# Elementwise steps of a four-layer network moved from VectorE and ScalarE to GpSimd, with the hand-written instruction order rewritten

## What is computed

```python
# layers 0 and 1: causal attention, a sign-weight linear, then a mixture of 16 experts (top 2) and a shared one
x = x + L2_xattn(ctx, layernorm(x), mask)    # query, key and value are each layer-normed after their projection:
    query = layernorm(q @ Wq + bq) * qn_scale + qn_bias     # key and value alike
x = x + L2_ffn(layernorm(x))                 # _bitlinear: rows scaled to 127 / max|row|, rounded, clipped
    xq = clip(round(x * scale), -128, 127) / scale
    hidden = silu(bitlinear(x, w_gate)) * bitlinear(x, w_up);  out = bitlinear(hidden, w_down)
x = x + L3_xattn(layernorm(x), ctx, ctx)     # keys and values are ctx itself, no projection
for blk in range(3):                         # L3_ffn, on h = layernorm(x)
    w = (q / 7.5 - 1.0) * scale              # 4-bit weights, a scale for each 16 of them, plus a low-rank term
    h = linear(gelu(layernorm(linear(h)) * gamma + beta)) + h
```

## Time and profile before

| | |
|---|---|
| median of three runs | 1198.68 us (1193.59 to 1200.58) |
| the profiled execution | 1198.55 us |
| its span, first to last instruction | 1196.6 us |
| busy: TensorE, VectorE, ScalarE, GpSimd | 1067.9, 945.9, 826.6, 488.3 us |
| as shares of the span | 89%, 79%, 69%, 41% |
| mean granted clock of TensorE | 0.972 of full speed |

### The profile page before, as it was taken

The page is one execution under the profiler, slowest core; times in us unless marked ns, Lnnn a source line. Parts: engine busy times, 40 slices in busy tenths (PEclk is TensorE's granted clock), DMA queues, the critical chain, the costliest instruction groups (busy, mean ns, idle before and its releaser), DMA issues.

```text
span 1196.6 us, 26279 instructions
## 1 busy us (share of the span) xinstructions
PE 1067.9 (89%) x8350; PEld 796.2 (67%) x8406; DVE 945.9 (79%) x3207; ACT 826.6 (69%) x1560; POOL 488.3 (41%) x1027
## 2 busy tenths in 40 slices
PE   6998999999999988899999988798899999988876
PEld 4676777777887765666677765366576766656654
DVE  3898888878555788877967798999999989898732
ACT  5777666657665666365667667457889798979953
POOL 6233356653122457657601144233334433423334
PEclk9999999999999999888999998999999999999988
DMA  7885332226777245303587752222203212121000
GB/s 221 260 275 180 87 101 71 85 76 189 218 211 213 89 121 140 85 14 116 150 259 229 233 167 80 56 69 82 82 19 87 72 54 81 53 63 54 10 10 18
DMA packets 102326, 140.03 MB, mean 117 GB/s; under 512 B 12336, under 2 KB 79792, under 8 KB 102192
## 3 DMA queue, kind: packets, MB, share of 16 engines
q1 hardware_dynamic: 99120, 129.97, 37.3%
q0 software_dynamic: 3072, 8.39, 2.2%
HBM read 65.43 MB, written 22.54 MB: 74 GB/s over the span
## 4 chain that ended last, share of the span: by engine, by line
PE 48%; DVE 20%; ACT 11%; DMA 7%; issue 6%; POOL 4%; SPq 3%; another core or an unknown queue 0%; DVEq 0%; ACTq 0%; POOLq 0%
PE ps L1516 10%; PE ps L1637 5%; PE ps L1536 4%; PE ps L1554 4%; PE ps L1729 4%; PE ps L1509 3%; DVE neg_max L2200 3%; PE ps L1523 3%; DVE ps L2196 3%; ACT probs L1945 3%; PE ps L1696 2%; DMA w<-in_expert 2%; ACT q_st L1960 2%; PE ps L1736 2%; DVE bn L2077 2%
## 5 line engine op out<-in xcount | busy, mean ns | idle before, releaser
L1945 ACT ACTIVATE probs<-ps 128x384 f32<-128x384 f32 (+1 forms) x512 | 263.5, 543 | 68.0 <-PE ps L1557 32.3
L1536 PE MATMUL ps<-k_st,q_st 96*128 96x256 bf16 (+1 forms) x1024 | 178.8, 265 | 19.4 <-DVE neg_max L2196 9.7
L1554 PE MATMUL ps<-q_st,k_st 104*128 104x256 bf16 (+1 forms) x1024 | 179.2, 263 | 14.8 <-ACT q_st L1960 6.7
L2200 DVE TENSOR_REDUCE neg_max<-ps 128x2 f32<-128x512 f32 x256 | 168.0, 679 | 11.7 <-PE ps L1536 4.9
L1960 ACT ACTIVATE q_st<-ps 8x1024 bf16<-8x1024 f32 x128 | 130.1, 1016 | 42.3 <-PE ps L1619 39.4
L2517 POOL TENSOR_SCALAR var_eps<-mv 128x2 f32<-128x2 f32 (+1 forms) x115 | 29.0, 252 | 298.0 <-DVE mv L2080 286.9
L2196 DVE CUSTOM_DVE_ANT_0 ps<-ps,diag_s 128x128 f32<-128x128 f32 (+1 forms) x384 | 123.3, 357 | 24.1 <-PE ps L1536 23.4
L1536 PEld LDWEIGHTS ps<-k_st,q_st 96*128 96x128 bf16 x1024 | 88.4, 100 | 70.3 <-DVE neg_max L2196 17.5
L1554 PEld LDWEIGHTS ps<-q_st,k_st 104*128 104x128 bf16 x1024 | 90.9, 99 | 60.3 <-issue 16.3
L1637 PE MATMUL ps<-probs,v 128*32 128x256 f32 (+1 forms) x2048 | 123.0, 359 | 4.7 <-ACT probs L1945 2.8
L2542 POOL CAST parts<-qf 128x512 bf16<-128x512 f32 x64 | 39.1, 612 | 205.2 <-DVE qf L2094 101.9
(11 more groups left out here) (270 smaller groups left out, 2545.8 us busy)
## 6 DMA issues: line engine op xcount, KB each, us to landing
k_st<-parts SPq DMA_DIRECT2D x192, 128.0 KB
q_st<-parts SPq DMA_DIRECT2D x192, 128.0 KB
w<-in_expert SPq DMA_DIRECT2D x62, 384.0 KB, 3.9
x_rows<-wo SPq DMA_DIRECT2D x10, 768.0 KB, 7.1
ctx_t<-in_ctx_t SPq DMA_DIRECT2D x16, 256.0 KB, 3.0
ring<-x_rows SPq DMA_DIRECT2D x31, 128.0 KB, 3.9
y_rows<-ring SPq DMA_DIRECT2D x31, 128.0 KB, 3.8
xn_t<-x_rows SPq DMA_DIRECT2D x31, 128.0 KB, 3.4
```

The source lines that it names most:

```text
L1536: last = mm(t[:, c0:c0 + n], head(q_st, r, h, KROWS, j * P, P), head(k_st, r, h, KROWS, 0, n), start=j == 0 or L != 2, stop=L != 2, skip_g ...
L1554: last = mm(t[:, j * S:j * S + n], head(k_st, r, h, KALL, j * P, P), head(q_st, r, h, KALL, skip, n), start=j == 0 or L == 3, stop=L == 3, ...
L1945: nc.scalar.activation(probs[:, (hg % 2) * HPG + h4, 0:width], tile_of(key)[:, 0:width], ACT.Exp, scale=SCALE).then_inc(*tile_drained(key))
L2200: V.tensor_reduce(neg_max[:, hg, h4, :], tile_of(key).rearrange("p (j t) -> p j t", j=SJ), AX.X, ALU.max, negate=True).then_inc(*tile_drai ...
```

## The change

Six things are moved to GpSimd, each with the same arithmetic: the norms of L2's queries, keys and values and of the blocks of the last feed-forward part (from ScalarE), and from VectorE the two rounding instructions of `quantise` and of `hidden_quant`, the two multiplications of `lora_add`, `value_scale`, and the values of layer 3. The moved steps get lanes' steps of their own (`quantise_round`, `hidden_round`, `lora_scale`, `v_copy`) and semaphores of their own (`ln_made`, `xq_round`, `hid_round`, `lora_made`). `low_load` waits for the last four expert tiles in place of the last one, and the first block that reads the 4-bit weights, whichever batch it belongs to, waits for them. The whole table `AT` is written anew, from the first microseconds on; it now ends at 1128.9 us.

```diff
 AT = (
...
 def low_rank(part):
...
         part.lora(n)
         yield
+        part.lora_scale(n)
+        yield
         part.lora_add(n)
...
     part.quantise(b)
     yield
+    part.quantise_round(b)
+    yield
     part.quantised(b)
...
     part.hidden_quant(T)
     yield
+    part.hidden_round(T)
+    yield
     part.down_turn(T)
...
     part.ctx_load(b)
     yield
-    part.v_take(3, b)
+    part.v_copy(3, b)
...
                 def block_in(n, b):
                     t = claim(pe, ("y", n, b))
-                    if b == 0:
+                    if n not in low_ranks_in:
+                        low_ranks_in.append(n)
                         wait_drained(pe, ("lora", 2 * n))
                         wait_drained(pe, ("lora", 2 * n + 1))
...
                 def apply(p, b):
-                    if p in ("k", "q", "v"):
-                        normalise(p, b, toks[p], toks[p])
-                        return
-                    if p[0] == "y":
-                        normalise(p, b, y_set(b)[0], y_set(b)[0])
+                    if p in ("k", "q", "v") or p[0] == "y":
                         return
...
+            def scaled(key, kind, T, rows):
+                G.tensor_scalar(rows, rows, rstd[:, kind, T:T + 1], shift[:, kind, T:T + 1], ALU.mult, ALU.add).then_inc(*ln_made.step(key))
...
+                def apply(p, b):
+                    if p in ("k", "q", "v") or p[0] == "y":
+                        pool.wait_ge(*ln_shift.at((p, b)))
+                        rows = y_set(b)[0] if p[0] == "y" else toks[p]
+                        for a in range(SJ):
+                            scaled((p, b, a), kind_of(p), b * SJ + a, rows[:, a, :])
+
+                def half_apply(n, a):
+                    pool.wait_ge(*ln_shift.at((("y", n, a), LAST)))
+                    scaled((("y", n), LAST, a), 0, LAST * SJ + a, y_set(LAST)[0][:, a, :])
+
+                def value_scale(b):
+                    pool.wait_ge(*ln_made.at(("v", b, SJ - 1)))
+                    G.tensor_tensor(toks["v"], toks["v"], spread(V_L2VS, SJ), ALU.mult).then_inc(*tok_made.step(b))
+                    before = same_side_before(2, b)
+                    pool.wait_ge(*pv_done.at((*before, HG - 1)))
+                    pool.wait_ge(*tok_made.at(b))
+                    for a in range(SJ):
+                        G.tensor_tensor(v[:, side(2, b), a, :, 0:DH], toks["v"][:, a, :].rearrange("p (h d) -> p h d", d=DH),
+                                        vec[:, V_L2VB, :].rearrange("p (h d) -> p h d", d=DH), ALU.add).then_inc(
+                            *v_ready.step((2, b, a)))
+
+                def v_copy(L, b):
+                    pool.wait_ge(*pv_done.at((*same_side_before(L, b), HG - 1)))
+                    r = side(L, b)
+                    pool.wait_ge(*ctxn_in[b % 4].at(b))
+                    for a in range(SJ):
+                        G.tensor_copy(v[:, r, a, :, 0:DH], h_of(b)[:, a, :].rearrange("p (h d) -> p h d", d=DH)).then_inc(
+                            *v_ready.step((L, b, a)))
+
+                def lora_scale(n):
+                    pool.wait_ge(*load[f"low{n}"].at(0))
+                    G.tensor_scalar(w3[:, n, :, :], w3[:, n, :, :].bitcast(I32), 1.0 / 7.5, -1.0, ALU.mult, ALU.add).then_inc(
+                        *lora_made.step(("deq", n)))
+                    pool.wait_ge(*lora_made.at(("deq", n)))
+                    pool.wait_ge(*lora_in.at((n, 3)))
+                    G.tensor_tensor(w3[:, n, :, :], w3[:, n, :, :], scale3, ALU.mult).then_inc(*lora_made.step(("mul", n)))
+
+                def quantise_round(b):
+                    flat = xn[:, NORMED["l2f"], :, :]
+                    pool.wait_ge(*quant.at(("dq_hid", b)))
+                    for a in range(SJ):
+                        T = b * SJ + a
+                        G.tensor_scalar(flat[:, a, :], flat[:, a, :], qscale[:, T:T + 1], ROUND, ALU.mult, ALU.add).then_inc(
+                            *xq_round.step((b, a)))
+                    if b:
+                        wait_filled(pool, ("xq", b - 1))
+                    for a in range(SJ):
+                        T = b * SJ + a
+                        pool.wait_ge(*xq_round.at((b, a)))
+                        G.tensor_scalar(xq[:, a, :], flat[:, a, :], ROUND, Q_MAX, ALU.subtract, ALU.min).then_inc(
+                            *xq_ready.step((b, a)))
+
+                def hidden_round(T):
+                    a = T % SJ
+                    h = hid[a]
+                    pool.wait_ge(*quant.at(("dqd", T)))
+                    G.tensor_scalar(h, h, hscale[:, T:T + 1], ROUND, ALU.mult, ALU.add).then_inc(*hid_round.step(T))
+                    pool.wait_ge(*hid_round.at(T))
+                    if T >= SJ:
+                        wait_filled(pool, ("ht", T - SJ))
+                    G.tensor_scalar(hid_q[:, a, :], h, ROUND, Q_MAX, ALU.subtract, ALU.min).then_inc(*hid_ready.step(T))
...
                 def low_load():
 
-                    wait_filled(sp, ("gd", NTILE - 1))
+                    for i in range(NTILE - RING, NTILE):
+                        wait_filled(sp, ("gd", i))
```

More of the change, by code:

```diff
@@ L1589, in token_turn @@
                     t = claim(pe, (what + "t", b))
-                    pe.wait_ge(*ln_done.at((what, b, SJ - 1)))
+                    pe.wait_ge(*ln_made.at((what, b, SJ - 1)))
                     turn_tokens(t, (what + "t", b), toks[what])
@@ L2146, in v_take @@
                     r = side(L, b)
[L2147 to L2162 removed]
+                    if (L, b) == (0, 0):
+                        dve.wait_ge(*load["vec1"].at(0))
+                        dve.wait_ge(*const_ready.at("last"))
+                    wait_filled(dve, ("v", L, b))
+                    for a in range(SJ):
+                        done = V.tensor_tensor(
+                            v[:, r, a, :, 0:DH],
+                            tile_of(("v", L, b))[:, a * D:(a + 1) * D].rearrange("p (h d) -> p h d", d=DH),
+                            vec1[:, V_BV[L], :].rearrange("p (h d) -> p h d", d=DH), ALU.add)
+                    done.then_inc(*tile_drained(("v", L, b)))
                 def token_bias(what, b):
@@ L2172, in token_bias @@
                     moments(what, b, toks[what])
-                def value_scale(b):
-                    dve.wait_ge(*ln_done.at(("v", b, SJ - 1)))
-                    V.tensor_tensor(toks["v"], toks["v"], spread(V_L2VS, SJ), ALU.mult).then_inc(*tok_made.step(b))
-                    before = same_side_before(2, b)
-                    dve.wait_ge(*pv_done.at((*before, HG - 1)))
-                    dve.wait_ge(*tok_made.at(b))
-                    for a in range(SJ):
-                        V.tensor_tensor(v[:, side(2, b), a, :, 0:DH], toks["v"][:, a, :].rearrange("p (h d) -> p h d", d=DH),
-                                        vec[:, V_L2VB, :].rearrange("p (h d) -> p h d", d=DH), ALU.add).then_inc(
-                            *v_ready.step((2, b, a)))
                 def ln(p, b):
```

67 lines of the change are left out of this document (14 added, 53 removed), and 1066 rows, old and new, of the table AT.

## The result

The changed kernel takes 1234.85 us (median of four, 1230.32 to 1243.76), against 1199.47 us for the kernel before in the same measurement. The ratio is 1.0314, 95% interval 1.0247 to 1.0382: 3% slower, where 2% faster was forecast. The profiled execution took 1243.76 us with a span of 1241.7, the longest of the four, so its differences to before are some 10 us larger than those of the medians.

A forecast was written before the change was run, and what follows sets the result against it. Bound: TensorE to 700 us, VectorE to 950, three nearly level engines to 1130, then dependency. Relief at chain shares, VectorE 15.7 plus ScalarE 9.1, is 24.8 us: 1198.55 - 24.8 = 1174 us, range 1150 to 1203.

The forecast's parts named there:

- the price of the second rounding: GpSimd's second rounding instruction: taken as any one-input operation, 1.1 us for 1024 columns, 0.5 for 256; upper bounds 2.54 and 0.73.
- the dependency time: Waits along moved steps: shorter norms save 9 us, 16 longer hidden roundings add 10 us, nearly cancelling and mostly covered.
- what a microsecond is worth: Relief counted at chain shares, VectorE 62.6 x 0.25 and ScalarE 57 x 0.16: 24.8 us gained; GpSimd's additions fall where it idles.
- The sum's second term, 10 us more on VectorE: VectorE's small copies of maxima wait for GpSimd's operations: 10 us more VectorE time, 2.5 us at its chain share.
- rival of the lock: VectorE's head-group copies wait on SBUF ports shared with GpSimd: 8 to 32 us given back, 1182 to 1206 us; chance 0.06.
- The busy times: Whole kernel, signs of being right: VectorE about 893 to 896 us busy, ScalarE 770, GpSimd 610 to 645.
- slower rival: New order of the first 16 items makes that stage 28 us later: 1202 to 1219, say 1211 us; chance 0.12.
- Its marker: First exponent of item (1, 7), at 487.9 us before: a start after 512 us decides for the slower rival.
- GpSimd's path: Norms, rounding and `value_scale` share GpSimd's in-order queue with `power`: gain only 8 to 12 us, say 1190 us; chance 0.12.
- TensorE as the bound: TensorE, 87 to 92% busy, absorbs the relief, so the time stays at 1198 us; chance 0.08.

The follow-up runs named there:

- rounds_alone: Table of before with only the two roundings moved to GpSimd, second one as subtract and minimum: 1259.73 us, 1.0564 of the kernel before.
- fast_round: Changed kernel with the second rounding as multiply by 1.0 and add, minimum with 127 left out: 1199.33 us, 1.0049 of the kernel before.
- order_alone: Changed kernel's new table with every moved instruction back on VectorE or ScalarE: 1251.54 us, 1.0442 of the kernel before.
- one_op: Changed kernel with the second rounding of hidden rows on GpSimd cut to the subtraction, minimum left out: 1223.35 us, 1.0214 of the kernel before.
- second_back: Changed kernel with the second instruction of both roundings back on VectorE, table still new: 1220.08 us, 1.0156 of the kernel before.
- round_back: Changed kernel with both instructions of both roundings back on VectorE, table still new: 1222.12 us, 1.0179 of the kernel before.
- fast_vl_back: `fast_round` with values and low-rank scaling back on VectorE: 1210.7 us, 1.0129 of the kernel before.
- old_prefix: Changed kernel with the order of before up to the first scores of item (1, 7), all moves kept: 1230.32 us, 1.0286 of the kernel before.
- prefix_fast: `fast_round` with the order of before up to the first scores of item (1, 7): 1199.56 us, 1.0025 of the kernel before.
- forms: Changed kernel with three rounds of ten GpSimd instruction forms on 1024 columns appended after all other work: 1.04 to 3.65 us each, total not compared.
- norms_alone: Table of before with only the 96 norms moved from ScalarE to GpSimd, right behind `power`: 1200.91 us, 1.0005 of the kernel before.

## Why the prediction was wrong

**The step that failed first: the price of the second rounding.** The prediction took 1.1 us for every one-input operation of 1024 columns, "nearer to the cast (one tensor read), with a little for the second scalar", and as upper bound two inputs, 2.54. The first rounding, the norms and the casts kept to that: 1.12, 0.56 to 0.57 (0.5 taken), 0.62 (0.65 taken). The second rounding took 3.69 us, above the upper bound, and 1.07 us for 256 columns where 0.73 was the bound. By the terms of the sum: norms 53.5 us (48 predicted), rounding of inputs 24.7 (16), of hidden rows 76.9 (35.2), `value_scale` 22.0 (21.8), `lora_scale` 11.4 (11.5), copies of values about 6 (6.9). GpSimd's busy time rose by 193.5 us, where 139 was the sum and 222 its upper end. The mistake was to bound a form that the trace did not show by the number of inputs only, with the operation left out of account. Changing nothing but the form takes back 0.0265 of the 0.0314 of loss, 32 of 38 us. So this term explains most of the loss. It doesn't explain why no gain came: with it put right the kernel is at 1.0049, not below 1.

The same wrong price stood in the dependency time. The prediction had 16 roundings longer by 0.6 us each, 10 us, "that other work mostly covers". The rounding of a hidden tile became 4.81 us long (1.12 + 3.69) where it was 1.585, that is 16 x 3.2 = 52 us in place of 10, and by `rounds_alone` nothing of the slow form was covered.

**The step that failed second: what a microsecond is worth.** Relief was counted at chain shares, VectorE 0.25 and ScalarE 0.16, which made 24.8 us, and the additions to GpSimd at 0.10 or, in the forecast itself, at nothing, because "GpSimd's additions lie where it now idles". With the fast form the sum on GpSimd is 140.1 us (628.4 less 488.3), just what was predicted, and the time is still 1.0049. So the gain of 24.8 us that stayed out, and the 6 us lost besides, are not a matter of the price. The runs show both halves of the mistake. ScalarE's relief, with its norms put on GpSimd, is worth nothing (1.0005 for 44 us less). And GpSimd's time on the roundings is not worth 0.10 but 0.6 on the new table and 1.1 on that of before (59 of 52.5 us). A reading that fits, argued and not isolated: the moved steps are links between two other engines, so their length can enter the path whole, whether GpSimd idles before or after. Its share in the chain rises by 83 us in `fast_round` (48 to 131), about what VectorE (239 to 227) and ScalarE (132 to 72) give up. A chain share is the average over an engine's old work; it says nothing of a step that is put in elsewhere.

**The sum's second term, 10 us more on VectorE,** was about right in size and wrong in place. The two lines of copies went from 31.5 and 29.5 us to 31.1 and 32.2, 2 us together. The rest came in other instructions, most in those that prepare the mask (7.9 to 11.1 us) and in the one that adds the experts' rows to x (15.4 to 18.7), of which one of two groups stands here, before and after:

```profile
L2328 DVE SCALAR_TENSOR_TENSOR x<-xn_t,weight,x 128x256 f32<-128x256 f32 x16 | 7.4, 480 | 2.3 <-DMA xn_t<-y_rows,dest 1.6
```

```profile
L2316 DVE SCALAR_TENSOR_TENSOR x<-xn_t,weight,x 128x256 f32<-128x256 f32 x16 | 10.2, 653 | 2.2 <-DMA xn_t<-y_rows,dest 1.5
```

All of VectorE's instructions, added up one by one, take 1140.4 us before and 1086.6 after; 62.4 of that were moved away, so those that stayed grew by 8.5 us, and by 10.7 in `fast_round`. In `order_alone`, with the new order and GpSimd's old work, nothing grew (1136.8 us for the same instructions as before). The rival of the lock thus has some 10 us of VectorE time to stand on, not 32; at its own shares of the chain that is 2 to 10 us. It can't be the main cause, but the 6 us that `fast_round` loses are of that size, and no run shows how much of them comes from it. The rule of the Trainium skill (SBUF — State Buffer, Who interferes with whom) is visible in the longest copy, 2297 ns across three instructions of GpSimd.

**The busy times.** VectorE's 901.0 us stands 5 to 8 above the forecast, ScalarE's 783.4 stands 13 above the 770. Added up one by one, its instructions fall from 911.9 to 855.0 us, just the 57 predicted; busy time counts two that overlap once, and by that measure the removed groups were 52.5 us and the fall is 43.2. Where instructions overlap, count times mean is too large.

**The slower rival.** Its marker came true, 514.3 us, past the 512. Yet it is not the main cause. In six kernels with the order of the changed kernel up to there (order_alone, one_op, second_back, round_back, fast_round, fast_vl_back) the exponent started at 513.6, 509.1, 515.6, 510.8, 500.0 and 503.9 us; with it 12 us later than the earlier trace rows, `fast_round` ends at 1.0049. And in the two kernels with the old order up to it the exponent came at 507.3 (`old_prefix`) and 503.1 (`prefix_fast`), later than in `fast_round`. The time of one instruction was a poor threshold: a late item is not late work.

A better measure is how many weight loads TensorE has made by 455 us, ahead of nearly all moved work. Eight traces with the new order (`forms` included) have 3478 to 3602, 3532 on average; twelve with the order of before have 3570 to 3634, 3596 on average. The 64 fewer are some 8 us at the 7.9 loads per us of `fast_round` from 400 to 455 us. The measure is rough, as the two orders don't do the same work first, and `fast_round` shows that the new order can be level. Restoring the old order gains 0.2 to 0.3% (`old_prefix` to the change, `prefix_fast` to `fast_round`), inside the intervals. So the rival is worth something between nothing and some 8 us, and that stays open.

**The other rivals.** GpSimd's path (1190) named the right engine and the right queue, but let it take most of the gain, not more than all. TensorE as the bound is refuted for the changed kernel: it idled more, 23 us, and ran 50 us more at the lower clock level. For `fast_round` and the single moves, whose times stand at 1.000 to 1.010, the data can't tell a bound by TensorE from a path of equal length around it.

**What stays open.** `order_alone` at 1.044 beside `fast_round` at 1.005 says that on the new table the moves are worth 3.9%; on the old one they cost 2.2%. That the table is written for the moves is clear; which of its places cost the 4.4% without them was not tried, and neither was why `second_back`, with the second rounding on VectorE, stays at 1.6% where the fast form on GpSimd comes to 0.5%. How much of the loss comes through the clock (117 us at the lower level in the change; 74 us in `fast_round`, whose mean granted clock is 0.969) and how much makes the clock fall can't be separated, since idle TensorE and a low clock came together in every kernel.

## What to carry to other kernels

Before moving an operation to GpSimd, measure that very form, operations and operands included: two instructions on the same tile differed by 3.3 times. A step between two engines can cost its whole latency on the new engine (here 0.6 to 1.1 us for each us of the roundings), not its share of a chain; relief of an engine that stands at a few per cent of the chain, or of one of several near-critical engines, can be worth nothing. And a hand-written order fits the placement it was written for: try each half alone, but expect the halves not to add.

## What the runs showed of the hardware

GpSimd's `tensor_scalar` has a fast and a slow group of forms. Per column, from the medians at 256 and 1024 columns in `fast_round`, `one_op` and the changed kernel: multiply-and-add (1045 - 404)/768 = 0.83 ns; subtraction alone (2784 - 859)/768 = 2.5 ns; subtract-and-minimum (3643 - 1070)/768 = 3.4 ns. The output type makes no difference (3640 and 3630 ns). By the Trainium skill (GPSIMD Engine Reference, 3.1 Elementwise — side-by-side cycle accounting, and 4.1 Engine selection) a body of up to two operations runs at 1.03 cycles per element, which at the engine's clock of 1.2 GHz by the same page (1. Specifications) would be 0.86 ns, an estimate; and an operation with one input goes at roughly line rate. The runs agree for multiply-and-add (0.83 ns) and for the cast (1037 ns for 1024 columns), and disagree by a factor of 3 to 4 for a subtraction, a minimum, and pairs of subtract and minimum or add and maximum.

A small VectorE copy can stand through several GpSimd instructions that follow each other without a gap: 2297 ns in the changed kernel and 2273 in `fast_round`, each ending within 0.04 us of the end of the third.

Executions of one kernel spread here by up to 1.4% (`norms_alone`, 1192.85 to 1209.41 us), and the profiled start of one instruction varied by 15 us (500.0 to 515.6) among seven kernels with the same order before it. A single profile of this kernel can't settle less than about 1%.
